# Attention with decayed scores and a small mixture of experts: the product of scores and values on fp32 operands in place of three fp16 products

## The reference, cut to what matters

```
csum    = cumsum(log_sigmoid(ftilde))
Dtilde  = (csum_i - csum_j, masked to j <= i) + itilde_j
D       = exp(Dtilde - max_j Dtilde)
Ctilde  = (q k^T) * D / 4
Htilde  = Ctilde v / (max(|sum_j Ctilde|, exp(-max_d)) + 1e-6)
x       = x + group_norm(Htilde) * gn_w + gn_b
x       = x + routed experts (2 of 8) + one gated shared expert, of layer_norm(x)
```

## Time and profile before

| | |
|---|---|
| median of three runs | 214.66 us (214.27 to 215.34) |
| span of the profiled execution, first to last instruction | 210.8 us |
| time around that span, median less span | 3.9 us |
| mean granted TensorE clock over the span | 0.862 |
| busiest engines by share of the span | PE 79%, DVE 75%, POOL 56%, PEld 50%, ACT 42% |
| chain that ended last, by engine | PE 38%, DVE 26%, POOL 14%, issue 9%, DMA 5%, ACT 5% |

### The profile page before, as it was taken

One profiled execution on the slowest core, in us unless ns is written; L12 is line 12 of the kernel. 1 busy time (PEld: TensorE's weight loads), 2 busy tenths in 40 slices (PEclk: granted clock), 3 DMA queues, 4 the chain that ended last, 5 costly groups with the idle time before them and its releaser, 6 DMA issues.

```text
span 210.8 us, 4540 instructions
## 1 busy us (share of the span) xinstructions
PE 165.8 (79%) x1682; PEld 106.2 (50%) x1682; DVE 158.6 (75%) x485; ACT 89.6 (42%) x156; POOL 117.7 (56%) x130
## 2 busy tenths in 40 slices
PE   0485864866339949897999899979899899788793
PEld 0372632635325626554665556546466656555461
DVE  6698827997897988698478868884896797766542
ACT  2164416315065432663364326542654743543620
POOL 8303369946976993397566825794672443161100
PEclk9995596559659985999669967996999999999999
DMA  6811499300023300016003400120000000000000
GB/s 179 248 48 33 114 218 213 62 0 3 0 67 78 105 14 3 0 36 110 6 0 62 91 4 0 66 84 3 0 28 2 3 25 3 0 26 5 25 0 25
DMA packets 15446, 10.48 MB, mean 50 GB/s; under 512 B 2416, under 2 KB 13312, under 8 KB 15424
## 3 DMA queue, kind: packets, MB, share of 16 engines
q1 hardware_dynamic: 14704, 9.11, 17.5%
q10 hardware_dynamic: 720, 1.08, 2.4%
HBM read 8.03 MB, written 1.11 MB: 43 GB/s over the span
## 4 chain that ended last, share of the span: by engine, by line
PE 38%; DVE 26%; POOL 14%; issue 9%; DMA 5%; ACT 5%; SPq 1%; ACTq 0%; DVEq 0%; POOLq 0%
PE bank L773 11%; PE bank L751 7%; PE bank L703 5%; POOL rstd L394 4%; POOL rs L398 4%; PE bank L762 3%; DMA mb<-m_scratch 3%; DVE xn L1061 3%; PE bank L677 3%; DVE hc L1142 2%; DMA xs<-in_x 2%; POOL dd L259 2%; DVE q L230 2%; PE bank L687 2%; DVE csum L941 1%
## 5 line engine op out<-in xcount | busy, mean ns | idle before, releaser
L773 PE MATMUL bank<-hc,w 128*128 128x256 f32 x144 | 44.9, 433 | 0.7 <-DVE hc L1147 0.7
L751 PE MATMUL bank<-xnT,w 128*128 128x256 f16 x240 | 35.3, 295 | 1.2 <-ACT hh L525 1.2
L525 ACT ACTIVATE hh<-bank 128x512 f32<-128x512 f32 (+1 forms) x40 | 22.1, 552 | 28.3 <-DVE hc L1142 17.0
L773 PEld LDWEIGHTS bank<-hc,w 128*128 128x128 f32 x144 | 26.2, 201 | 10.2 <-issue 5.3
L394 POOL TENSOR_TENSOR rstd<-ve,const 128x16 f32<-128x16 f32 x8 | 23.2, 2904 | 13.4 <-DVE ve L1029 13.4
L751 PEld LDWEIGHTS bank<-xnT,w 128*128 128x128 f16 x240 | 23.7, 104 | 9.5 <-issue 2.9
L1142 DVE TENSOR_TENSOR hc<-bank,hh 128x512 f32<-128x512 f32 x32 | 21.9, 684 | 5.3 <-PE bank L762 2.3
L703 PEld LDWEIGHTS bank<-v,ct 64*64 64x64 f16 x768 | 17.6, 127 | 10.8 <-issue 9.7
L388 POOL TENSOR_TENSOR yw<-y,gnw 128x256 f32<-128x256 f32 x8 | 5.5, 683 | 28.1 <-DVE y L1023 28.1
L703 PE MATMUL bank<-v,ct 64*64 64x17 f16 x768 | 20.1, 185 | 0.6 <-DVE ct L262 0.6
L259 POOL TENSOR_TENSOR dd<-dd,mb 128x1024 f32<-128x1024 f32 (+1 forms) x8 | 19.4, 2424 | 2.1 <-DMA mb<-m_scratch 1.6
(11 more groups left out here) (135 smaller groups left out, 319.0 us busy)
## 6 DMA issues: line engine op xcount, KB each, us to landing
mb<-m_scratch SPq DMA_DIRECT2D x12, 256.0 KB, 4.8
xs<-in_x SPq DMA_DIRECT2D x4, 256.0 KB, 3.9
cx<-in_ctx SPq DMA_DIRECT2D x4, 256.0 KB, 4.2
qblk<-qT SPq DMA_DIRECT2D x64, 16.0 KB, 2.3
mb<-m_scratch ACTq DMA_DIRECT2D x4, 256.0 KB, 7.9
w<-in_w SPq DMA_DIRECT2D x2, 512.0 KB, 9.0
out<-ob SPq DMA_DIRECT2D x8, 128.0 KB, 1.8
const<-in_const SPq DMA_DIRECT2D x1, 176.5 KB, 4.3
```

Of the source, the lines that this page charges most:

```text
L525: A.activation(hh[:, n % 2].rearrange("p e s -> p (e s)")[:, 0:w], pH[n % 2][:, 0:w], ACT.Silu).then_inc(silu_ready, 1)
L751: ins = pe.matmul(pH[n % 2][:, j * S:(j + 1) * S], w12[:, u, 2 * s + j], xnT2[:, v], start=(i == 0), stop=(i == 2))
L773: ins = pe.matmul(pY[:, 0:S], w2[:, e], hc[:, n % 2, j], start=(e == 0), stop=(e == E))
```

## The change

The intra product takes ct (the weights) and the values, now vx with its 17th column of ones, in fp32 as they stand: one matmul per head and half instead of three. ACT's `ct_high` and `values_high`, DVE's `low_half` and POOL's `values_low` are gone, with one memset. DVE's centring writes into vx with a stride of 17, and POOL reads the values from there. PE waits per tile for ct itself, and once per batch for the centred values; the wait that kept ct2 from being overwritten (for intra of batch b - 2) is now DVE's, ahead of writing ct.

```
@@ pool
-            G.memset(v2[:, 0, :, :, HD:VW], 1.0).then_inc(ones_set, 1)
-            G.memset(v2[:, 1, :, :, HD:VW], 0.0).then_inc(ones_set, 1)
+            G.memset(vx[:, :, :, HD:VW], 1.0).then_inc(ones_set, 1)
...
-            values_low(0)
             exponent(1)
...
-            values_low(1)
             weighted_values(2)
...
-                if b % 2 == 0 and b // 2 + 1 < NG:
-                    values_low(b // 2 + 1)
@@ act
-            values_high(0)
             q_copy(2)
-            ct_high(0)
...
-            ct_high(1)
             q_copy(3)
-            values_high(1)
...
                 silu(f, 2)
-                if b + 1 < B:
-                    ct_high(b + 1)
-                if b % 2 == 0 and b // 2 + 1 < NG:
-                    values_high(b // 2 + 1)
                 silu(f, 3)
@@ tensor, intra
                 if t == 0 and hs[0] == 0:
-                    pe.wait_ge(ct_lo, b + 1)
-                    pe.wait_ge(v_lo, b * TPB // GRP + 1)
+                    pe.wait_ge(vc_ready, b * TPB // GRP + 1)
+                    pe.wait_ge(ones_set, 5)
+                if hs[0] == 0:
+                    pe.wait_ge(ct_ready, TPB * b + t + 1)
...
-                    for i, (u, v) in enumerate(PAIR):
-                        for half in range(2):
-                            r = slice(half * C, (half + 1) * C)
-                            ins = pe.matmul(pP[r, t * HW + h * VW:t * HW + (h + 1) * VW],
-                                            ct2[r, k, u, t, h, :], v2[r, v, b * TPB + t, h, :],
-                                            start=(i == 0), stop=(i == 2))
+                    for half in range(2):
+                        r = slice(half * C, (half + 1) * C)
+                        ins = pe.matmul(pP[r, t * HW + h * VW:t * HW + (h + 1) * VW],
+                                        ct[r, k, t, h, :], vx[r, b * TPB + t, h, :],
+                                        start=True, stop=True)
@@ vector
-                V.scalar_tensor_tensor(vc[:, a].rearrange("p t (h d) -> p (t h) d", h=H), over(vsum[:, hs], HD),
+                V.scalar_tensor_tensor(vx[:, a, :, 0:HD].rearrange("p t h d -> p (t h) d"), over(vsum[:, hs], HD),
...
                 dve.wait_ge(scores_done, TPB * b + t + 1)
+                if b >= 2:
+                    dve.wait_ge(intra_done, TPB * (b - 1))
...
-            low_half(0)
             states(0)
...
             gate_tokens(1)
-            low_half(1)
             group_norm(0)
...
                     token_stats(b)
-                if ahead:
-                    low_half(b + 1)
                 if b < B:
                     layer_norm(b)
```

More of the change, by code:

```diff
@@ L75, in xattn_moe @@
         vsum = sb("vsum", [P, NT * H])
-        vc = sb("vc", [P, NT, D])
         q = sb("q", [P, NT, D])
@@ L80, in xattn_moe @@
         kT2 = sb("kT2", [P, 2, B * S], f16)
-        v2 = sb("v2", [P, 2, NT, H, VW], f16)
+        vx = sb("vx", [P, NT, H, VW])
         wg = sb("wg", [2 * H, 3 * D])
@@ L119, in xattn_moe @@
         ct = sb("ct", [P, 2, TPB, H, C])
-        ct2 = sb("ct2", [P, 2, 2, TPB, H, C], f16)
         kw = sb("kw", [P, 2, 4, H, VW])
@@ L183, in xattn_moe @@
         qT_copied = sem("qT_copied")
-        v_hi, v_lo = sem("v_hi"), sem("v_lo")
         wgT_done, wg_split = sem("wgT_done"), sem("wg_split")
@@ L195, in xattn_moe @@
             sem("decay_ready"), sem("xg_ready")
-        scores_done, ct_ready, ct_hi, ct_lo = sem("scores_done"), sem("ct_ready"), sem("ct_hi"), sem("ct_lo")
+        scores_done, ct_ready = sem("scores_done"), sem("ct_ready")
         state_done, cst_ready, intra_done, inter_done, y_ready = sem("state_done"), sem("cst_ready"), \
@@ L259, in minus_m @@
             return eng.tensor_tensor(ddf, ddf, mb[:, k, ts].rearrange("p t h i -> p (t h i)"), ALU.subtract)
-        def ct_low(eng, k):
-            return eng.tensor_tensor(
-                ct2[:, k, 1].rearrange("p t h i -> p (t h i)"), ct[:, k].rearrange("p t h i -> p (t h i)"),
-                ct2[:, k, 0].rearrange("p t h i -> p (t h i)"), ALU.subtract)
         QBANK = (bank[0], bank[1], bank[5], bank[5])
@@ L340, in inverse_root @@
                 G.tensor_tensor(rs1[:, s], ve1[:, s], neghalf[:, 0:GRP], ALU.pow).then_inc(rstd1_ready, 1)
-            def values_low(g):
-                pool.wait_ge(v_hi, g + 1)
-                a = slice(g * GRP, (g + 1) * GRP)
-                G.tensor_tensor(v2[:, 1, a, :, 0:HD], vc[:, a].rearrange("p t (h d) -> p t h d", h=H),
-                                v2[:, 0, a, :, 0:HD], ALU.subtract).then_inc(v_lo, 1)
             def masked_g(b):
@@ L371, in weighted_values @@
                     G.tensor_tensor(
-                        kw[:, k, v, :, 0:HD], vc[:, a].rearrange("p (h d) -> p h d", h=H),
+                        kw[:, k, v, :, 0:HD], vx[:, a, :, 0:HD],
                         tok[:, T_WK + v, b, :].rearrange("p (h o) -> p h o", o=1).to_broadcast([P, H, HD]),
@@ L451, in _ @@
             A.preload_act_table_set("natural_log_exp_and_others")
-            def values_high(g):
-                act.wait_ge(vc_ready, g + 1)
-                a = slice(g * GRP, (g + 1) * GRP)
-                A.copy(v2[:, 0, a, :, 0:HD], vc[:, a].rearrange("p t (h d) -> p t h d", h=H))\
-                    .then_inc(v_hi, 1)
             def ctx_high(g):
@@ L501, in decay @@
                 A.activation(f, f, ACT.Exp).then_inc(decay_ready, 1)
-            def ct_high(b):
-                k = b % 2
-                act.wait_ge(ct_ready, TPB * (b + 1))
-                if b >= 2:
-                    act.wait_ge(intra_done, TPB * (b - 1))
-                A.copy(ct2[:, k, 0].rearrange("p t h i -> p (t h i)"),
-                       ct[:, k].rearrange("p t h i -> p (t h i)")).then_inc(ct_hi, 1)
             def xn_high(b):
@@ L543, in _ @@
             decay(0)
-            act.wait_ge(ones_set, 6)
-            values_high(0)
+            act.wait_ge(ones_set, 5)
             q_copy(2)
-            ct_high(0)
             act.wait_ge(w1_in, 32)
@@ L694, in intra @@
                 if t == 0 and hs[0] == 0:
-                    pe.wait_ge(ct_lo, b + 1)
-                    pe.wait_ge(v_lo, b * TPB // GRP + 1)
+                    pe.wait_ge(vc_ready, b * TPB // GRP + 1)
+                    pe.wait_ge(ones_set, 5)
+                if hs[0] == 0:
+                    pe.wait_ge(ct_ready, TPB * b + t + 1)
+                if t == 0 and hs[0] == 0:
                     if b >= 1:
@@ L1147, in weigh @@
                     V.tensor_tensor(hc[:, n % 2, 0], pB[:, 0:S], up[:, :], ALU.mult).then_inc(hc_ready, 1)
-            def low_half(b):
-                dve.wait_ge(ct_hi, b + 1)
-                if b >= 2:
-                    dve.wait_ge(intra_done, TPB * (b - 1))
-                ct_low(V, b % 2).then_inc(ct_lo, 1)
             for t in range(TPB):
                 scores_decay(0, t)
-            low_half(0)
             states(0)
```

## The result

The changed kernel takes 204.51 us, median of four runs (203.22 to 207.55), against 214.47 us for the kernel before in the same session (four runs, 214.16 to 215.34). The ratio is 0.9496 [0.943, 0.9563], and 0.9496 x 214.47 is 203.7 us: about 5% faster, a gain 3 us larger than predicted. (The ratio leaves out runs that are over 1.5% longer than the fastest of their kernel, here the 207.55.) The profiled execution took 203.22 us, with a span of 201.4 and a mean clock of 0.89.

The account below looks back on a forecast made before the run. Iterations 1 to 4 bound by the DVE-POOL chain up to the transpose, then PE; 5 and 6 by PE; prologue by DVE and POOL. Terms -2.5, -3.6, +2.2, -3.9 sum to -7.8: 206.9 us, range 203.8 to 212.8.

Parts of the forecast that it names:

- The root and the waits: POOL's L398 takes 0.71 us without L262 beside it, xn 0.9 us earlier in iterations 1 to 4: -3.6 us.
- The product: At L703, fp32 pairs of 55 ns make each quarter 0.09 us longer, 20 quarters on the path: +2.2 us.
- The clock: Shorter PE waits before the transposes remove part of the low clock in iterations 2 to 4: -3.9 us, bounds 0 and -5.5.
- The stretch after iteration 1 stays in any case: The low clock behind iteration 1 was said to remain; half of iteration 2's 1.3 + 0.6 us was taken as won.
- the stretch of iteration 3: Low clock behind iteration 3's wait: 0.8 of 2.1 us put as won, plus 0.6 in the next hidden matmuls.
- The prologue: Up to y(1), 1.5 us from L961's earlier end and 1.0 from the second low half: -2.5 us, bounds 1.2 and 3.9.
- POOL's sequence moves up by the 1.2 us: In the prologue, one values_low less moves POOL up, so L961's end before y(0) moves 1.2 to 2.7 us, 1.5 taken.
- The time around the span: The 3.9 us between the 210.8 us span and the 214.66 us median lie outside the instructions and stay.
- The clock as before: Rival, chance 0.25: the waits shrink but the low clock stretches stay, -3.1 us, 211.6 us.
- the long root: Rival, chance 0.07: something other than L262 stretches POOL's root, so waits and clock stay, +0.5 us, 215.2 us.
- the halves one after another: Rival, chance 0.08: the fp32 product's two halves no longer go together, a quarter takes 0.88 us, +4.5 us, 219 us.
- the pair at fp16's price: Rival, chance 0.05: an fp32 pair takes 32 ns as in fp16, a quarter 0.25 us, 202.5 us.

Follow-up runs that it names:

- low_half_back: Changed kernel with an unread DVE subtraction of 128x1024 (two SBUF inputs) back between token statistics and xn in six iterations; 213.15 us, ratio 0.9948.
- one_input: Changed kernel with an unread DVE reduction of 128x1024 (one SBUF input) between token statistics and xn in six iterations; 204.72 us.
- product_only: Kernel before with the intra product on fp32 operands, every split still made and waited for; 218.38 us, ratio 1.0174.
- high_thrice: Changed kernel with ACT's fp16 high halves of scores and values multiplied three times, low halves left out; 202.14 us, ratio 0.9424.
- centre_late2: Second series of the changed kernel with the centring moved behind the last expert's weighing; 199.05, 198.66, 198.47 and one 465.38 us, ratio 0.9255.
- before_busy: Kernel before with four unread matmuls added where PE waits for xn in iterations 1 to 4; 209.13 us, ratio 0.9751.
- second profile: Changed kernel measured and profiled once more, no edit, against the kernel before; 203.69 us, ratio 0.9505.
- pool_back: Changed kernel with one unread POOL subtraction of 128x512 back in the prologue, between mask and exponent of batch 1; 206.49 us, ratio 0.9562.
- centre_late: First series of the changed kernel with the centring moved behind the last expert's weighing; 204.34, 203.28, 198.21 and 203.26 us.
- late_busy: Changed kernel with the centring behind the last weighing and four unread matmuls at each of two PE waits; 199.11 us, ratio 0.9277.

## Why the prediction was right or wrong

The measured 203.7 us lies 0.1 below the stated range of 203.8 to 212.8. The mechanism came as predicted. Two terms were mis-sized, the prologue's and the time around the span, and the clock's came out right in sum only.

**The root and the waits: right.** L398 at 0.71 was predicted for all batches and is there; from the token statistics to the transposes it takes 3.9 us in place of 4.8 in iterations 1 to 4, the 0.9 each that I counted. low_half_back and one_input show the cause: a DVE instruction with two SBUF inputs beside the root makes it 1.61 us, one of the same length with one input leaves it at 0.71. (That it is the inputs and not what is written rests on POOL's L356 above, not on a run of its own.)

**The product: right.** +0.09 us a quarter was predicted. A quarter of the kernel after at full clock, the window of L664 (PE, PEld busy, clock, DMA, GB/s):

```profile
111.00:112.30 1.30, 0.64 (x16) 0.54 (x16) 1.00 0.11 26
```

0.64 against 0.55 in the earlier trace rows. The loads' 0.54 less the last one's 0.135 make 7 steps of 58 ns between pairs (55 predicted), so the two halves do go together. Iterations 5 and 6 are 0.39 us longer (0.36 predicted), as in product_only and, the other way round, in high_thrice. By the rule of the Trainium skill's TensorEngine Tiling (Array Packing), section Performance Considerations, that each matmul has some 60 cycles of overhead, a quarter would be an estimated 0.2 us shorter than before; it is 0.09 longer.

**The clock: right in sum, wrong in its places.** Iterations 1 to 4 together gained 5.8 us, 6.0 predicted. Take off 3.6 for the roots and add back 1.5 for the product, and what is left for the clock is 3.7, against the 3.9 taken; it is a remainder, not a measurement. But two steps failed. "The stretch after iteration 1 stays in any case" is wrong: with a wait of 0.19 us no low clock follows y(2), and iteration 1 gained 1.7 instead of 0.2 (y(2) came at 79.3, not near 82.6). And the stretch of iteration 3, which I let half vanish with the wait before the transposes, got another cause: POOL waited for mb, L922 took 2.15 us beside its exponent, PE waited 1.33 us for hc, and iteration 4 gained 1.2 instead of 2.7. I had named DVE's centring as what "holds up the last expert there", but took 0.8 of that iteration's 2.1 us as won all the same; centre_late2 shows 3.2 us still to be had there. That low clock comes with PE's waits, and mostly goes when they are filled or removed, is shown from both sides by before_busy and low_half_back.

**The prologue: the term that was mis-sized.** -2.5 us was taken; from ct(0) to y(1) it is -3.6 (-4.0 in the second profile). The step that failed is that DVE's way to y(0) is bounded by "POOL's sequence moves up by the 1.2 us": POOL did not go on, it waited for mb, and DVE used the gap. y(0) came 4.4 us earlier, not 1.5. The second low half was rightly priced (1.0; 18.41 - 17.12 = 1.3 with pool_back), but between y(0) and y(1) the changed kernel is still 0.8 us slower than before, since DVE's little L1045 ran into POOL's L403 and took 2.47 us instead of 0.17, which cost 2.1 (19.21 - 17.12). Together: 4.4 + 1.3 - 2.1 = 3.6. Had I put the engines' lines side by side at their new times, with the transfer's landing (34.8) held fixed, both would have been seen.

**The time around the span: wrong.** "The 3.9 us between them lie outside the instructions and stay" took the median less the span for a fixed cost. In all twelve profiled executions whose time is known, time less span is 1.8 us (203.22 - 201.4 here), and so it is in the timed runs of before beside them (214.57 us with a span of 212.8). The profiled execution of before thus took some 212.6 us, 2 below its median: of the 3.9 us, 2.1 were no time around the span but work in longer spans, which the rows did not show and which does not simply stay. With 1.8 the sum of 203.0 gives 204.8 us, and 203.2 was measured in the profiled execution. Of the 1.6 between them, 0.8 are the start's transfers, which is luck, and 1.1 the prologue; iterations 1 to 6 take off 0.3. From there to the ratio it goes so: the two profiled executions are 9.4 us apart, the ratio says 10.8, because executions of before are mostly 2 us longer than its profiled one and those of after some 0.5. Where in the kernel those 2 us lie, no profile shows.

**The rivals.** The clock as before (211.6) falls with one low stretch behind 64.8 us (116.0 to 122.8) where before had four, the long root (215.2) with 0.71 us, the halves one after another (219) and the pair at fp16's price (202.5) with 58 ns.

## What to carry to other kernels

Look at which DVE and POOL instructions overlap before counting either engine's time: here a hidden DVE instruction of 1.2 us, in six iterations, cost 7 to 9.5 us of kernel, by 0.9 us on a tiny POOL instruction, a PE wait of about 1 us or more, and the low clock after it. When work is removed, hold the transfers fixed and lay the engines' lines out anew: twice here POOL came to wait for the same transfer, and its next instruction then met another one of DVE. And add to a span the time outside it of the same execution, not the median's. And where low clock follows a gap on PE, try unread matmuls in it: before_busy is two lines and brought half of this change's gain.

## What the runs showed of the hardware

- What stretches what. POOL's 128x2 root took 0.71 us alone, 0.71 beside a DVE reduction of 128x1024 and 1.61 beside a DVE subtraction of 128x1024 that reads two operands. The root ended 0.57 us behind the subtraction (low_half_back, 113.78 and 114.35). (GPSIMD Engine Reference in the Trainium skill, section Key points, says that contention is with DVE instructions in a 2-port perf mode or with two SBUF inputs; on the two inputs the trace agrees.)
- It goes the other way too, and I had not weighed it: beside POOL instructions of 1.2 to 3.3 us, four DVE normalisations (TENSOR_SCALAR, one tensor input) took 2.95 to 4.07 us in place of 1.11, one on 128x16 numbers 2.47 in place of 0.17, and the centring 1.58 to 3.03 in place of 0.69. (VectorE: DVE Perf Modes in the Trainium skill, section What auto-detection actually checks, says that a single-source instruction with source and destination in SBUF, and with even or equal outermost dimensions, takes a mode that the page's table marks as using both read ports. That would cover the TENSOR_SCALARs; no run here moved their operands to test it.)
- Two fp32 64x64 matmul records in opposite corners of the array start 7 ns apart (changed kernel, at 111.3), and a pair takes 58 ns at full clock; fp16 pairs start 3 ns apart and take 32 (before, at 139.6). A fp32 matmul is two records, so its pair costs 116 ns in all.
- PE waits of 1.33 us (changed kernel, 115.3) and 1.81 us (centre_late, 74.6) were followed by 6.8 and 10.2 us of low clock, waits of 0.2 to 0.6 us before the transposes by none right behind. The length alone does not decide: 1.15 us in iteration 1 of before_busy was followed by none either, and a wait of 0.85 us for hc by none in the changed kernel (77.9) but by 3.4 us in pool_back (82.3). Every profile but late_busy's has a wait of 1.26 or 1.27 us behind y(7); in four of the twelve no low clock follows it.
- An early low stretch is not all loss: in the changed kernel, with the clock low up to 64.8, PE reached the transposes of iteration 1 so late that it waited 0.19 us and kept full clock up to 116.0; in centre_late low clock ended at 60.9, PE waited 1.81 us and then ran 10.2 us at the low level.
